# Node-query gate loop: the GpSimd addition of two product buffers is given up, and TensorE sums all four in two halves

## The chip, the cores and the metric

The kernel runs on one core of a Trainium2 chip, as one program. The metric is the device time in microseconds (us) from start to end; lower is better. The kernel before takes 1924.17 us, the median of 3 runs (1922.68 to 1926.9).

## The reference, cut to what matters

The program is eight layers on 256 nodes of 768 features. The change lies in the first one, `L0_gnn`, which runs a relational graph convolution and a query gate twice:

```python
hg = einsum('bnf,gf->bng', h3, Wg[:, :F])            # nodes:   8 graphs x 32 nodes x 768
qg = einsum('blf,gf->blg', q, Wg[:, F:]) + bg        # queries: 8 graphs x 64 queries x 768
attn = sigmoid(hg[:, :, None, :] + qg[:, None, :, :])   # 8 x 32 x 64 x 768
qi = einsum('bnlf,blf->bnf', attn, q)                # sum over the 64 queries
alpha = sigmoid(h3 @ Wq[:, :F].T + qi @ Wq[:, F:].T + bq)
hn = alpha * tanh(qi) + (1 - alpha) * h3
```

`attn` has 12.6 million elements in each of the two passes (l = 0, 1), and every one needs an addition, a sigmoid, a multiplication by q and a place in the sum over the queries.

## The kernel before

**Tiling.** A pass of the gate is a loop of 96 steps: 24 groups G (j = G // 8 is one of three blocks of 256 features, b = G % 8 is one graph) of four steps t, each for 16 of the graph's 64 queries. A step holds 128 partitions (8 nodes x 16 queries) x 1024 elements (4 sets of nodes x 256 features), in float32.

**One step.** TensorE fills two PSUM banks with node + query sums (`fill_pe`, L850: two bf16 products of 512 columns against a selection matrix; the rows come from the buffer `gate_rows`, kept as three bf16 parts). ScalarE takes the sigmoid into a product buffer (L969). VectorE multiplies by the query values `gate_queries`, in place (L1018, the helper's line is L120). TensorE sums over the queries with a selection matrix of 32 columns (`query_sum_pe`, L860: four column tiles of 256 columns, float32, one "quad" below; the profile records two matmuls for each float32 product), accumulating in bank 4 over all graphs of a block.

**Buffers.** There are two fill buffers in PSUM, so filling n waits for sigmoid n - 2 (`attended`), and eight product buffers (two groups), so the sigmoids of group G wait for the sums of group G - 2 (`qi_ps`, L967). The query values stand in three buffers (RBUF), so those of group G + 3 are requested once group G is multiplied (`weighed`, L728).

**The sum before.** GpSimd adds the second buffer of a group to the first (`gate_pool`, L1031), and TensorE sums three buffers, behind the third filling of the next group (L927 to L934). In the last group TensorE sums all four (L935).

**Beside the loop.** TensorE also works off products of the gate's weights (`beside`, L898): 36 products with the nodes and 24 with the query sums, of 128x256 float32 each, two or three behind the first filling of every group. The last 12 (features of block 2) come behind the loop (L943 to L949).

**Blocks.** Behind the sum of a block ScalarE copies it out, TensorE turns it (`turn_qi_pe`, in groups 9 and 17 behind the second filling, and behind the loop) and ScalarE copies it again.

**Transfers.** SyncE's queue issues all of them in program order: `gate_sp` (L793) the query parts to DRAM and back as rows, three buffers of query values, the node parts to DRAM and back; then a weight matrix of 2304 KB (L1041, L1045); then `gate_loop_sp` (L816), for each group the query values of G + 3 and the rows of G + 8, and in group 16 one more weight matrix.

The order of work on each engine is written out by hand; engines meet by semaphores (`mark`, `at`) alone.

Of the kernel before, what the change touches and what calls it, by code (L numbers as in the profile page):

```python
# [10 lines left out]
ALU = mybir.AluOpType  # L11
# [4 lines left out]
T = 256  # L16
TC = T // P
D = 768
DC = D // P
# [20 lines left out]
class Counts:  # L40
# [20 lines left out]
    def at(self, name, key=0):  # L61
        if self.counted:
            return self.sem(name), self.value[name, key]
        return self.sem(name), 1
# [104 lines left out]
def build(nc, dram, out_dram):  # L169
    ctx = ExitStack()  # L170
    with ctx:
# [61 lines left out]
        def loaded(key):  # L233
            return at(f"slot{counts.slot.get(key, 0)}_loaded", key)
# [558 lines left out]
        def gate_sp(q, l):  # L793
            load(q, ("Wgh", l), dram["L0_gnn_Wg"][0])
            load(q, ("Wqh", l), dram["L0_gnn_Wq"][0])
            load(q, ("Wqi", l), dram["L0_gnn_Wq"][1])
            counts.slot["work", l] = q.turns.pop(0)[0]
            at_wgh = [key for slot, key in q.turns].index(("Wgh", l))
            q.turns.append((q.turns.pop(at_wgh)[0], ("Wqi", l)))
            q.turns.append((counts.slot["work", l], ("Wqi", l)))  # L800
            if l == 0:
                for b in range(QB):
                    if b % 2 == 0:
                        query_parts_sp(q, b // 2)
                    query_rows_sp(q, 0, b)
            for G in range(RBUF):
                queries_sp(q, l, G)
            for b in range(QB):
                q.wait_ge(*(at(f"gate_rows_{b % 2}", (l, b - 2, "nodes") if b >= 2 else (l, QB - 2 + b, "queries"))))
                if b == QB // TC:  # L810
                    q.wait_ge(*at("gate_rows_1", (l, b - 1, "nodes")))
                if b % (QB // TC) == 0:
                    node_parts_sp(q, l, b // (QB // TC))
                node_rows_sp(q, l, b)
# [61 lines left out]
        def gate_pe(pe, l):  # L876
            wgh, wqh, wqi = (w3(unit((n, l)), DC, D) for n in ("Wgh", "Wqh", "Wqi"))
            pe.wait_ge(*loaded(("Wgh", l)))
            for c in range(TC):
                if l == 0 and c:  # L880
                    pe.wait_ge(*at("split_rest", NQ - 2))
                for k in range(DC):
                    if c == 0:
                        pe.wait_ge(*at("hidden", (l, k)))
                    for h in range(2):
                        t = pe.mm(PS[:, hidden_bank(c) + h, 0:HALF], hT[:, k, c * P:(c + 1) * P],
                                  wgh[:, k, h * HALF:(h + 1) * HALF], k == 0, k == DC - 1)
                t.then_inc(*(mark("unit_free", ("Wgh", l)) if c else mark("node_ps", (l, "rows"))))

            def hidden_product(o, k):  # L890
                return pe.mm(PS[:, gate_bank(o), o % 2 * T:(o % 2 + 1) * T], wqh[:, k, o * P:(o + 1) * P], hT[:, k, :],
                             k == 0 and o % 2 == 0, False)

            def query_product(o, f):
                return pe.mm(PS[:, gate_bank(o), o % 2 * T:(o % 2 + 1) * T], wqi[:, f, o * P:(o + 1) * P], qiT[:, f, :],
                             False, f == DC - 1 and o % 2 == 1)

            def beside(i):  # L898
                if i < DC * DC:
                    if i == 2 * DC:  # L900
                        pe.wait_ge(*at("split_rest", (l, TC - 1, 1)))
                    t = hidden_product(i // DC, i % DC)
                    if i == DC * DC - 1:
                        t.then_inc(*mark("unit_free", ("Wqh", l)))
                else:
                    f, o = divmod(i - DC * DC, DC)
                    pe.wait_ge(*at("qi_act", (l, "T", f // 2)))
                    query_product(o, f)

            pe.wait_ge(*at("kept", "gate_sel"))  # L910
            pe.wait_ge(*loaded(("Wqh", l)))
            pe.wait_ge(*loaded(("Wqi", l)))
            for n in range(STEPS):
                G, t = divmod(n, NQL)
                j, b = divmod(G, QB)
                if t == 0:
                    pe.wait_ge(*at(f"gate_rows_{b % 2}", (l, G, "nodes")))
                fill_pe(pe, l, n)
                if t == 0:
                    for i in range((5 * G + 1) // 2, (5 * G + 6) // 2):  # L920
                        beside(i)
                elif t == 1 and b == 1 and j:
                    pe.wait_ge(*at("qi_act", (l, "sb", j - 1)))
                    for f in range(2):
                        m = turn_qi_pe(pe, f, QI_BANK, f * TILE)
                    m.then_inc(*mark("qi_ps", (l, "turned", j - 1)))
                elif t == 2 and G:  # L927
                    if b == 1 and j:
                        pe.wait_ge(*at("qi_act", (l, "T", j - 1)))
                    pe.wait_ge(*at("folded", (l, G - 1)))  # L930
                    pe.wait_ge(*at("weighed", (l, NQL * G - 1)))
                    for u in (0, 2, 3):
                        m = query_sum_pe(pe, l, G - 1, u)
                    m.then_inc(*mark("qi_ps", (l, G - 1)))  # L934
            for u in range(NQL):  # L935
                pe.wait_ge(*at("weighed", (l, STEPS - NQL + u)))
                m = query_sum_pe(pe, l, GROUPS - 1, u)
            m.then_inc(*mark("qi_ps", (l, GROUPS - 1)))
            pe.wait_ge(*at("qi_act", (l, "sb", NREL - 1)))
            for f in range(2):  # L940
                turn_qi_pe(pe, f, 2 * f, 0).then_inc(*mark("qi_ps", (l, "turned", NREL - 1 + f)))
            pe.wait_ge(*at("qi_act", (l, "T", NREL - 1)))
            for o in range(DC):  # L943
                query_product(o, DC - 2)
            pe.wait_ge(*at("qi_dve", (l, "T")))
            for o in range(DC):
                t = query_product(o, DC - 1)
                if o % 2:
                    t.then_inc(*(mark("node_ps", (l, o // 2)) if o < DC - 1 else mark("unit_free", ("Wqi", l))))  # L949

        def gate_act(a, l):
            for c in range(TC):
# [75 lines left out]
                v.then(v.tt(gth[:, o2, :], gth[:, o2, :], galpha[:, o2, :], ALU.mult))  # L1028
                v.tt(hT[:, o2, :], hT[:, o2, :], gth[:, o2, :], ALU.add).then_inc(*mark("gated", (l, g)))

        def gate_pool(g, l):  # L1031
            for G in range(GROUPS - 1):
                w = [products(l, NQL * G + t) for t in range(2)]
                g.wait_ge(*at("weighed", (l, NQL * G + 1)))
                g.tt(w[0], w[0], w[1], ALU.add).then_inc(*mark("folded", (l, G)))


        def L0_gnn_sp(q):
            start_sp(q)
            gate_sp(q, 0)  # L1040
# [31 lines left out]

        def L0_gnn_pool(g):
            norm_pool(g, "L0_gnn")
            for l in range(2):
                gate_pool(g, l)

        def L0_gnn_dve(v):
            start_dve(v)
# [2559 lines left out]
```

## Time and profile before

| | us |
|---|---|
| median of 3 runs | 1924.17 |
| profiled execution, its own time | 1920.13 |
| its span (first to last instruction) | 1918.0 |
| gate loop, pass 0: first to last multiplication | 168.3 to 330.4 |
| gate loop, pass 1 | 434.6 to 595.7 |
| TensorE matmul busy, whole span | 1730.7 (90%) |
| VectorE busy | 708.6 (37%) |
| ScalarE busy | 438.5 (23%) |
| GpSimd busy | 177.0 (9%) |

Engines in the profile: PE is TensorE's matmuls, PEld its weight loads, DVE VectorE, ACT ScalarE, POOL GpSimd, SPq the transfers that SyncE issues. The page's busy shares are means over eight layers; the change touches the two gate loops, some 160 us each, and these are to be read by themselves. The mean granted clock of TensorE over the span is 0.975.

### The profile page before, as it was taken

How to read it: one execution, taken by the hardware profiler on the slowest of the kernel's cores; microseconds unless marked ns; L12 is line 12 of the kernel's file. 1: busy time of each engine (PE TensorE's matmuls, PEld its weight loads, DVE VectorE, ACT ScalarE, POOL GpSimd, SP SyncE). 2: the span in 40 equal slices, each digit the busy share in tenths (PEclk: the TensorE clock that was granted, in tenths of full speed). 3: DMA queues.
4: the chain of work that ended last, by engine and by line, in shares of the span. 5: the costliest groups of instructions: out<-in, count | busy, mean ns of one | idle time of the engine just before them, and what ended most of it. 6: DMA issues, size and time to landing. Idle time of an engine off the chain costs nothing.

```text
span 1918.0 us, 26881 instructions
## 1 busy us (share of the span) xinstructions
PE 1730.7 (90%) x11856; PEld 1043.3 (54%) x11856; DVE 708.6 (37%) x1179; ACT 438.5 (23%) x816; POOL 177.0 (9%) x81
## 2 busy tenths in 40 slices
PE   7997867997767999999999998887999899999999
PEld 4674433573435655567764443333566555766666
DVE  4325998008997222154321000001423232234220
ACT  0014555115663111043311000000521010131110
POOL 0002443004441000000000000000002000000000
PEclk9999899999999999989989999999999999999999
DMA  9216653617544677730358999999734336212650
GB/s 376 99 45 210 149 142 122 246 46 197 143 156 163 237 309 297 284 144 6 143 197 356 418 428 429 428 428 429 300 149 168 114 135 261 83 66 108 264 223 18
DMA packets 80748, 408.25 MB, mean 213 GB/s; under 512 B 9768, under 2 KB 50240, under 8 KB 58992
## 3 DMA queue, kind: packets, MB, share of 16 engines
q1 hardware_dynamic: 76112, 402.41, 55.0%
q10 hardware_dynamic: 4512, 4.03, 0.7%
q8 instruction: 98, 1.61, 0.3%
q14 instruction: 26, 0.21, 0.0%
HBM read 400.85 MB, written 5.51 MB: 212 GB/s over the span
## 4 chain that ended last, share of the span: by engine, by line
PE 69%; DVE 13%; DMA 12%; issue 4%; ACT 2%; POOL 0%; SPq 0%; DVEq 0%; ACTq 0%
PE banks L114 67%; DVE weight_ring L120 10%; DMA weight_ring<-in_L_ffn_c_fc_dram 7%; PE banks L117 2%; DMA weight_ring<-in_L_gnn_W_in_dram 2%; DMA weight_ring<-in_L_ffn_c_proj_e_dram 1%; ACT weight_ring L148 1%; DVE stat L266 1%; DMA gate_queries<-in_L_gnn_query_rep_dram 1%; DVE xn_tok L125 0%; DMA node_parts<-gate_node_parts 0%; DMA ident<-in_c_ident_dram 0%; DVE xT L137 0%; DVE stat L268 0%; DVE rgat_xr L137 0%
## 5 line engine op out<-in xcount | busy, mean ns | idle before, releaser
L120 DVE TENSOR_TENSOR weight_ring<-weight_ring,gate_queries 128x1024 f32<-128x1024 f32 x192 | 308.2, 1675 | 17.4 <-ACT weight_ring L148 16.2
L114 PE MATMUL banks<-weight_ring,xT 128*128 128x384 f32 x864 | 292.3, 490 | 2.4 <-DVE rgat_xr L137 1.5
L114 PEld LDWEIGHTS banks<-weight_ring,xT 128*128 128x128 f32 x864 | 161.9, 191 | 109.6 <-issue 9.0
L148 ACT ACTIVATE weight_ring<-banks 128x1024 f32<-128x1024 f32 x192 | 185.5, 1026 | 134.5 <-PE banks L114 134.4
L120 POOL TENSOR_TENSOR weight_ring<-weight_ring 128x1024 f32<-128x1024 f32 x46 | 150.3, 3266 | 429.2 <-DVE weight_ring L120 429.2
L114 PE MATMUL banks<-xT,weight_ring 128*128 128x256 f32 x792 | 182.2, 385 | 3.2 <-ACT x_tok L151 3.2
L114 PEld LDWEIGHTS banks<-xT,weight_ring 128*128 128x128 f32 x792 | 153.3, 194 | 31.2 <-issue 7.3
L114 PE MATMUL banks<-weight_ring,selrow 128*32 128x256 f32 x1168 | 81.5, 413 | 79.3 <-DVE weight_ring L120 79.1
L114 PE MATMUL banks<-weight_ring,r_xd 128*32 128x384 f32 (+1 forms) x2304 | 142.7, 406 | 1.1 <-DVE r_xd L124 0.6
L114 PE MATMUL banks<-weight_ring,moe_xdT 128*64 128x384 f32 x720 | 122.0, 489 | 21.7 <-DMA weight_ring<-in_L_ffn_c_fc_dram 20.7
L114 PE MATMUL banks<-gate_rows,selrow 96*128 96x512 bf16 x384 | 112.5, 406 | 12.0 <-ACT weight_ring L148 6.8
L114 PEld LDWEIGHTS banks<-weight_ring,r_xd 128*32 128x32 f32 x2304 | 76.6, 110 | 64.2 <-issue 54.5
L137 DVE COPY y_tok<-banks 128x384 f32<-128x384 f32 x32 | 17.8, 557 | 248.7 <-PE banks L117 248.7
L114 PEld LDWEIGHTS banks<-weight_ring,selrow 128*32 128x32 f32 x1168 | 40.8, 114 | 116.8 <-issue 95.7
L114 PEld LDWEIGHTS banks<-weight_ring,moe_xdT 128*64 128x64 f32 x720 | 50.6, 137 | 89.6 <-issue 54.9
L114 PE MATMUL banks<-weight_ring,y_tok 128*64 128x384 f32 x504 | 85.9, 490 | 10.9 <-DMA weight_ring<-in_L_ffn_c_proj_e_dram 10.9
L148 ACT ACTIVATE moe_h_tok<-banks 128x384 f32<-128x384 f32 x32 | 15.7, 491 | 265.9 <-PE banks L114 265.9
L114 PE MATMUL banks<-weight_ring,r_hT 128*32 128x192 f32 (+1 forms) x1152 | 73.2, 407 | 1.0 <-ACT r_hT L151 1.0
L114 PEld LDWEIGHTS banks<-gate_rows,selrow 96*128 96x128 bf16 x384 | 30.2, 101 | 77.7 <-issue 33.3
L114 PEld LDWEIGHTS banks<-weight_ring,y_tok 128*64 128x64 f32 x504 | 34.3, 137 | 55.5 <-issue 38.9
L114 PEld LDWEIGHTS banks<-weight_ring,r_hT 128*32 128x32 f32 x1152 | 36.7, 110 | 37.2 <-issue 34.0
L120 DVE TENSOR_TENSOR selrow<-banks,gate_node_parts 128x384 f32<-128x384 f32 x16 | 8.5, 555 | 129.9 <-ACT gate_node_parts L151 99.9
(371 smaller groups left out, 1856.3 us busy)
## 6 DMA issues: line engine op xcount, KB each, us to landing
weight_ring<-in_L_ffn_c_fc_dram SPq DMA_DIRECT2D x30, 2304.0 KB, 23.8
weight_ring<-in_L_ffn_c_proj_e_dram SPq DMA_DIRECT2D x21, 2304.0 KB, 28.3
gate_queries<-in_L_gnn_query_rep_dram SPq DMA_DIRECT2D x48, 512.0 KB, 4.0
weight_slot_heads<-in_L_ffn_c_proj_e_dram SPq DMA_DIRECT2D x9, 2304.0 KB, 28.3
weight_ring<-in_L_ffn_w_gate_dram SPq DMA_DIRECT2D x8, 2304.0 KB, 9.4
weight_ring<-in_L_ffn_w_up_dram SPq DMA_DIRECT2D x8, 2304.0 KB, 9.1
weight_ring<-in_L_ffn_w_down_dram SPq DMA_DIRECT2D x8, 2304.0 KB, 9.2
weight_ring<-in_L_ffn_w_dram SPq DMA_DIRECT2D x16, 1152.0 KB, 8.2
```

Source lines behind the costliest of these rows:

```text
L114: return self.e.matmul(out, lhsT, rhs, start=start, stop=stop)
L117: return self.e.transpose(out, src, self.ident[0:n, 0:n])
L120: return self.e.tensor_tensor(out, a, b, op)
L137: return self.e.tensor_copy(out, a)
L148: return self.e.activation(out, a, f, **kw)
L266: t = v.e.bn_stats(half_stats[:, c, h, :], src[:, 2 * c + h, :])
```

## The change

GpSimd's addition goes (`gate_pool` and the wait `folded`). TensorE sums the first two buffers of the last group behind the second filling of a group, and the other two behind the fourth; in groups 9 and 17, where the second filling is followed by the turn of a block, all four behind the fourth. Six of the `beside` products go ahead of the loop, 52 into it (13 per 6 groups), and two behind it. Behind the loop the last 12 products are ordered by pairs of output chunks, so that the first pair is complete after four. In pass 0 SyncE requests the three buffers of query values before the query rows of graphs 6 and 7.

```diff
@@ gate_sp: transfers ahead of the loop
                 for b in range(QB):
+                    if b == QB - 2:
+                        for G in range(RBUF):
+                            queries_sp(q, l, G)
                     if b % 2 == 0:
                         query_parts_sp(q, b // 2)
                     query_rows_sp(q, 0, b)
-            for G in range(RBUF):
-                queries_sp(q, l, G)
+            else:
+                for G in range(RBUF):
+                    queries_sp(q, l, G)
@@ gate_pe
             pe.wait_ge(*loaded(("Wqh", l)))
+            if l == 0:
+                pe.wait_ge(*at("split_rest", (NQ - 1, "biased")))
+            for i in range(DC):
+                beside(i)
             pe.wait_ge(*loaded(("Wqi", l)))
             for n in range(STEPS):
...
                 fill_pe(pe, l, n)
                 if t == 0:
-                    for i in range((5 * G + 1) // 2, (5 * G + 6) // 2):
+                    for i in range(DC + 13 * G // 6, DC + 13 * (G + 1) // 6):
                         beside(i)
-                elif t == 1 and b == 1 and j:
+                if t == 1 and b == 1 and j:
...
-                elif t == 2 and G:
+                elif t == 1 and G:
+                    pe.wait_ge(*at("weighed", (l, NQL * G - 3)))
+                    for u in range(2):
+                        query_sum_pe(pe, l, G - 1, u)
+                elif t == 3 and G:
                     if b == 1 and j:
                         pe.wait_ge(*at("qi_act", (l, "T", j - 1)))
-                    pe.wait_ge(*at("folded", (l, G - 1)))
                     pe.wait_ge(*at("weighed", (l, NQL * G - 1)))
-                    for u in (0, 2, 3):
+                    for u in range(0 if b == 1 and j else 2, NQL):
                         m = query_sum_pe(pe, l, G - 1, u)
                     m.then_inc(*mark("qi_ps", (l, G - 1)))
...
             m.then_inc(*mark("qi_ps", (l, GROUPS - 1)))
+            for i in range(DC + 13 * GROUPS // 6, (DC - 2 + DC) * DC):
+                beside(i)
...
-            for o in range(DC):
-                query_product(o, DC - 2)
-            pe.wait_ge(*at("qi_dve", (l, "T")))
-            for o in range(DC):
-                t = query_product(o, DC - 1)
-                if o % 2:
-                    t.then_inc(*(mark("node_ps", (l, o // 2)) if o < DC - 1 else mark("unit_free", ("Wqi", l))))
+            for g in range(DC // 2):
+                for f in (DC - 2, DC - 1):
+                    if f == DC - 1:
+                        pe.wait_ge(*at("qi_dve", (l, "T")))
+                    for o in (2 * g, 2 * g + 1):
+                        t = query_product(o, f)
+                t.then_inc(*(mark("node_ps", (l, g)) if g < DC // 2 - 1 else mark("unit_free", ("Wqi", l))))
@@ gate_pool, and its call in L0_gnn_pool
-            for G in range(GROUPS - 1):
-                w = [products(l, NQL * G + t) for t in range(2)]
-                g.wait_ge(*at("weighed", (l, NQL * G + 1)))
-                g.tt(w[0], w[0], w[1], ALU.add).then_inc(*mark("folded", (l, G)))
```

## Rows read from the trace of the kernel before

**Rows 1.** The chain of waits, 0 to 700 us, in pass 0: start, length, what.
```profile
257.31 4.30 DVE weight_ring L120 x4
...
261.61 2.40 issue
```

**Rows 2.** The instructions on the product buffers, 224 to 297 us: durations min/median/max in ns.
```profile
L120 DVE TENSOR_TENSOR weight_ring<-weight_ring,gate_queries x44: 1210/1212/3372, 223.8 to 294.2; 128x1024 f32<-128x1024 f32 x44
...
L120 POOL TENSOR_TENSOR weight_ring<-weight_ring x11: 3263/3266/3268, 226.2 to 293.2; 128x1024 f32<-128x1024 f32 x11
```

**Rows 3.** The timeline, 244 to 258 us: start, length, engine, operation, [idle before it].
```profile
244.14 1.50 PE L114 MATMUL banks<-weight_ring,selrow 128*32 128x256 f32 x24 [2.02 <-DVE weight_ring L120]
...
245.57 1.04 PE L114 MATMUL banks<-gate_rows,selrow 96*128 96x512 bf16 x4
...
246.45 1.46 PE L114 MATMUL banks<-xT,weight_ring 128*128 128x256 f32 x6
...
247.74 1.07 PE L114 MATMUL banks<-gate_rows,selrow 96*128 96x512 bf16 x4
...
252.92 3.77 ACT L148 ACTIVATE weight_ring<-banks 128x1024 f32<-128x1024 f32 x4 [2.60 <-PE banks L114]
```

**Rows 4.** The timeline, 428 to 485 us: VectorE behind one transfer, in pass 1.
```profile
457.09 10.18 DVE L120 TENSOR_TENSOR weight_ring<-weight_ring,gate_queries 128x1024 f32<-128x1024 f32 x7 [1.17 <-DMA gate_queries<-in_L_gnn_query_rep_dram]
```

**Rows 5.** The timeline at the end of pass 1, 584 to 650 us.
```profile
581.07 14.61 DVE L120 TENSOR_TENSOR weight_ring<-weight_ring,gate_queries 128x1024 f32<-128x1024 f32 x9
...
591.29 1.50 PE L114 MATMUL banks<-weight_ring,selrow 128*32 128x256 f32 x24 [2.02 <-DVE weight_ring L120]
...
592.72 0.60 PE L114 MATMUL banks<-gate_rows,selrow 96*128 96x512 bf16 x2
...
593.26 1.07 PE L114 MATMUL banks<-weight_ring,selrow 128*32 128x256 f32 x16
...
596.44 0.59 ACT L151 COPY selrow<-banks 128x512 f32<-128x512 f32 x1 [2.05 <-PE banks L114]
...
597.08 1.16 PE L114 MATMUL banks<-ident,selrow 128*128 128x128 f32 x8 [0.71 <-ACT selrow L151]
...
598.25 5.45 PE L114 MATMUL banks<-gate_qiT,weight_ring 128*128 128x256 f32 x24
...
602.95 0.69 DVE L120 TENSOR_TENSOR xn_tok<-xn_tok,gate_queries 128x512 f32<-128x512 f32 x1 [2.81 <-ACT gate_queries L148]
```

**Rows 6.** Three stretches: busy us (and starts) of each engine, granted clock, DMA share, GB/s.
```profile
177.00:183.70 6.70, 6.27 (x38) 3.21 (x38) 5.46 (x5) 2.63 (x3) 3.27 (x1) 0.75 0.82 263
257.50:284.30 26.80, 18.95 (x156) 10.35 (x157) 26.80 (x17) 16.12 (x18) 13.06 (x4) 1.00 0.54 138
350.00:361.00 11.00, 11.00 (x36) 6.50 (x35) 0.00 (x0) 1.50 (x2) 0.00 (x0) 1.00 1.00 417
```

**Rows 7.** The chain of waits, 0 to 700 us: two transfers that the work waited for.
```profile
157.54 6.29 DMA node_parts<-gate_node_parts
...
445.73 11.34 DMA gate_queries<-in_L_gnn_query_rep_dram
```

**Rows 8.** Transfers issued at 179.1, 449.3, 170.0 and 297.6 us: KB, us to landing.
```profile
gate_queries<-in_L_gnn_query_rep_dram SPq DMA_DIRECT2D x1, 512.0 KB, 10.6
...
gate_queries<-in_L_gnn_query_rep_dram SPq DMA_DIRECT2D x1, 512.0 KB, 11.7
...
node_parts<-gate_node_parts SPq DMA_DIRECT2D x1, 576.0 KB, 3.3
...
gate_queries<-in_L_gnn_query_rep_dram SPq DMA_DIRECT2D x1, 512.0 KB, 4.0
```

**Rows 9.** The timeline of pass 0: first filling, the request behind group 2, last multiplication.
```profile
166.53 0.59 PE L114 MATMUL banks<-gate_rows,selrow 96*128 96x512 bf16 x2 [4.20 <-DMA gate_rows<-node_parts]
...
190.42 0.35 SPq L154 DMA_DIRECT2D gate_queries<-in_L_gnn_query_rep_dram  x1
...
329.17 1.23 DVE L120 TENSOR_TENSOR weight_ring<-weight_ring,gate_queries 128x1024 f32<-128x1024 f32 x1 [1.38 <-ACT weight_ring L148]
```

More of the change, by code:

```diff
@@ L1029, in gate_dve @@
                 v.tt(hT[:, o2, :], hT[:, o2, :], gth[:, o2, :], ALU.add).then_inc(*mark("gated", (l, g)))
-        def gate_pool(g, l):
-            for G in range(GROUPS - 1):
-                w = [products(l, NQL * G + t) for t in range(2)]
-                g.wait_ge(*at("weighed", (l, NQL * G + 1)))
-                g.tt(w[0], w[0], w[1], ALU.add).then_inc(*mark("folded", (l, G)))
         def L0_gnn_sp(q):
@@ L1074, in L0_gnn_pool @@
             norm_pool(g, "L0_gnn")
-            for l in range(2):
-                gate_pool(g, l)
         def L0_gnn_dve(v):
```

## The prediction

> **What bounds the kernel now.** I read the page's busy shares first (in the table above). They say TensorE, but they are means over eight layers; the change touches two loops of 160 us, so these are read alone. The chain of waits, cut to a loop, is VectorE's: in a group of 6.70 us it holds four multiplications for 4.30 us and an "issue" stretch of 2.40 us that belongs to VectorE too [rows 1]. The windows confirm it: between 257.5 and 284.3 us VectorE is busy for all 26.8 us, TensorE for 18.95, ScalarE for 16.12, at a granted clock of 1.00 and a DMA share of 0.54 [rows 6].
>
> Then the instructions on the product buffers: the same multiplication takes 1212 ns as a rule and 3372 ns at most; one GpSimd addition lasts 3266 ns [rows 2]. Their records overlap a little, so I take the spacing s of a fast one and x of the slow one from two counts. A group is 3s + x = 6.70. Seven multiplications behind the transfer at 457.09, one of them slow, take 10.18 us, the last one with its full 1.21: 5s + x = 8.97 [rows 1, 2, 4]. So s = 1.135 and x = 3.295: VectorE loses 2.16 us in each group in which GpSimd works, 23 groups in each of two passes. Without that, VectorE needs 4s = 4.54 us for a group.
>
> **The change part by part.**
>
> *GpSimd's addition goes.* VectorE's bound falls from 6.70 to 4.54 us. If nothing else bounded, 46 x 2.16 = 99 us would go. It doesn't all go, for two reasons below.
>
> *TensorE's bill for a group, the term that decides.* At the high clock: two fillings start 0.88 us ahead of what follows them (245.57 to 246.45), so 0.44 each; six records, that is three beside products, 1.29 us (246.45 to 247.74), 0.43 each [rows 3]. Three quads last 1.50, two 1.07: 0.43 each [rows 5]. Around the quads there are gaps. Three quads are 1.29 us, but the filling behind them starts after 1.43 (244.14 to 245.57 and 591.29 to 592.72): 0.14 on the way out. A filling is 0.44, but the quads behind that of 592.72 start after 0.54, with their data ready: 0.10 on the way in [rows 3, 5]. Now: 4 x 0.44 + 3 x 0.43 + 2.5 x 0.43 + 0.24 = 4.37 us, inside 6.70, with an idle time of 2.02 ahead of the sum [rows 3]. After: 4 x 0.44 + 4 x 0.43 + 13/6 x 0.43 + 2 x 0.24 = 1.76 + 1.72 + 0.93 + 0.48 = 4.89 us. That is above VectorE's 4.54, so TensorE becomes the bound. Bounds: 4.55 if the gaps are hidden in a full queue (then VectorE bounds), 5.37 if each gap is twice as long, since the way in rests on one place. I take 4.89, from the nearest rows.
>
> The Trainium skill, TensorEngine Tiling (Array Packing), Key Properties, says that a change of tiling mode drains TensorE; here the mode (128x32 against full width) changes four times in a group in place of two. It agrees with the two gaps, gives no figure, and speaks against splitting the sum in halves: with one block of four quads the bill would be 4.65.
>
> *Do the waits fit in between?* ScalarE needs 3.77 us for four sigmoids [rows 3], so it isn't the bound. A sigmoid starts 0.65 us behind its filling (252.27 to 252.92 in the loop, the filling of rows 3 one group on). The quads behind the second filling wait for the second multiplication of the group before, which is two fillings further back than what they'd wait for behind the fourth. The quads behind the fourth filling wait for the fourth multiplication, and ScalarE, which needs them to refill the buffers, is by then two or three steps ahead of VectorE. Queued behind a quad that waits are the next filling, its sigmoid and all beside products; with VectorE 0.35 us per group faster than TensorE that wait is empty after the first groups. Cost taken: 0, ends 0 and 0.3 us a group.
>
> *Turns of a block, groups 9 and 17.* All four quads stand behind the fourth filling there, beside 1.16 us of turning [rows 5], less the gaps of one block: about 1.2 us each where TensorE bounds; 2.4 per pass.
>
> *The first three groups win nothing.* In pass 1 the query values of group 3 are issued at 445.73, behind the weight matrix, and land 11.34 us later, at 457.07; VectorE starts group 3 at 457.09, on that landing [rows 4, 7]. Neither transfer is moved in pass 1, and its issue follows SyncE's rows, not VectorE. Faster, VectorE would want it at about 449 (434.6 + 3 x 4.9). So group 3 starts at 457.1 as before. Group 4's values land at 449.3 + 11.7 = 461.0 [rows 8], in time for 457.1 + 4.6. In pass 0 the values requested at 179.1 land 10.6 us later, at 189.7 [rows 8]; group 3 started at 190.4, where SyncE's next request shows group 2 done [rows 9]. The new place of the first three requests spares the node parts the transfers beside them: 6.29 us in place of 3.3 [rows 7, 8]; but they now delay the query parts and the rows of graphs 6 and 7, for which SyncE waits before the node parts. I take 0.5 us (ends -1 and 3): group 3 at 189.2. Later the lead of a request is two groups, 9.8 us, against a landing of 4.0 [rows 8], and the DMA share of 0.54 x 6.70 = 3.6 us a group stays under 4.89.
>
> *From group 3 to the end.* When group 3 starts, TensorE has filled up to step 17 of 0 to 95 and waits for group 3's second multiplication, 2.3 us off. Then 78 fillings, 19.25 groups to the start of the last: 19.25 x 4.89 = 94.1; the turns 2.4; from the last filling 0.65 + 1.02 + 0.1 + 1.21, and 0.7 of queueing: 3.7. Sum 102.5 us. Now it is 595.68 - 457.09 = 138.6 in pass 1 [rows 4, 5] and 330.40 - 190.4 = 140.0 in pass 0 [rows 9].
>
> *The clock.* Where TensorE idled, the granted clock fell (0.75 over 177.0 to 183.7, half of it at the low level of 1.2 GHz); under unbroken work it stays 1.00 (350 to 361) [rows 6]. The stall ahead of group 3 will bring one such fall per pass: half of 6.7 us at half speed loses 1.7; I take 1.5.
>
> So pass 1 ends at 457.1 + 104.0 = 561.1, 34.6 earlier; pass 0 at 189.2 + 104.0 = 293.2, 37.2 earlier.
>
> *Behind the loop.* Two beside products (0.86) stand in the 0.64 from ScalarE's copy to the turn (596.44 to 597.08) and its release before: 0.15 late, ends 0 and 0.5. The first output pair is complete after 4 products in place of 8, 1.7 us earlier; but the pass goes on only when TensorE is through all 12 (5.45 us from 598.25) or VectorE's chain, begun at 602.95, is done [rows 5]. I take a gain of 1.1 for each pass, ends 0 and 2. Both together: 1.9 us.
>
> *Six products ahead of the loop.* In pass 0 TensorE idles 4.20 us there [rows 9], and they take 2.6: hidden. In pass 1 they delay the first filling by about 1.5 us, covered by the wait for group 3.
>
> **Sum.** 37.2 + 34.6 + 1.9 = 73.7 us. The profiled execution took 1920.13, so 1846.4; it lies 4.0 under the median of the runs, which gives 1924.2 - 73.7 = 1850.5. What follows starts at PE-bound stages or at loads released by them, and moves with them. I forecast 1850.
>
> **Rivals.**
> A. *The gaps close, VectorE bounds.* 4.54 in place of 4.89: 2 x 19.25 x 0.35 = 13 us less, and the clock's 3 perhaps: 1835. For it: the gaps may be the wait's own cost. Against: at 591.29 nothing was waited for on the way out [rows 5]. 15%.
> B. *More gap, or late query values.* At 5.37 a group 18.5 us more: 1869. If landings of 11.7, as beside a weight matrix [rows 8], held for the whole loop, two groups would take 11.7, one 5.85: 2 x 21 x 0.96 = 40 more, 1890; against it the 4.0 of the later ones. Together 14%.
> C. *Slower than before: TensorE at its low level for the loop.* All products last twice as long: 8.8 + 0.5 = 9.3 us a group, 2 x 21 x 2.6 = 109 us more: 2033. It is slower than before once a share f of over 0.41 of the loop is at the low level (4.89 + 4.4 f > 6.70). For it: the falls now. Against: they follow idle times of 2 us a group, which the change takes away, and 350 to 361 holds 1.00 [rows 6]. 3%.
> D. *VectorE isn't slow for GpSimd's sake.* Then 6.70 stays and the time with it: 1922. Against: exactly one multiplication in each group is slow, as one addition is made in each [rows 1, 2]. The Trainium skill, SBUF — State Buffer, Who interferes with whom, says that a VectorE instruction with two SBUF inputs and a GpSimd one that reads SBUF exclude each other on a shared port; the trace agrees, 1.135 + 2.16 = 3.3 being the GpSimd record's 3.27. 2%.
> The forecast has 66%.
>
> **Range and chances.** What a measurement of this kernel can tell from no change is about 0.2%, 4 us. A to B's first half and the ends of the small terms (start -1 to 3, tail 4, waits 0.3 x 40) give 1834 to 1872, with under 2 in 10 outside. Faster: all but C and D, 0.95; same 0.02; slower 0.03.
>
> **What would show it.** No multiplication over 1.3 us. From group 3 on a period near 4.9, TensorE busy for nine tenths or more at clock 1.00, and quads in two blocks with 0.1 and 0.14 of gap; a period of 4.55 with VectorE unbroken is A, one over 5.2 is B. VectorE idle ahead of group 3 in both passes, released by the query values' DMA; if it isn't there, the start-up term was wrong. Loops from group 3 to the end of about 104 us.

## The result, and the profile after

The kernel after takes **1856.88 us**, the median of 4 runs (1853.85 to 1860.77); the kernel before took 1923.6 in the 4 runs counted with it (1922.68 to 1926.9). The ratio is 0.9651, with a 95% interval from 0.9627 to 0.9676: 3.5% faster, 66.7 us. The prediction was 1850 within 1834 to 1872. The profiled execution took 1854.55 us, its span is 1852.4.

The chain of waits, 0 to 700 us (start, length, what): the loops, which were VectorE's [rows 1], are now unbroken stretches of TensorE, ahead of each a wait for query values.

```profile
179.76 12.44 DMA gate_queries<-in_L_gnn_query_rep_dram
...
194.64 98.72 PE banks L114 x878
...
412.22 11.01 DMA gate_queries<-in_L_gnn_query_rep_dram
...
425.67 97.62 PE banks L114 x878
```

The instructions on the product buffers, 225 to 285 us (durations min/median/max in ns), against [rows 2]: no slow multiplication is left.

```profile
L120 DVE TENSOR_TENSOR weight_ring<-weight_ring,gate_queries x49: 1218/1220/1226, 224.4 to 284.4; 128x1024 f32<-128x1024 f32 x49
```

The timeline of one group in that loop, against [rows 3]. Each gap is read as the distance of two starts less the work between (a half sum is 16 records, a filling 2, a beside product 2).

```profile
237.34 1.07 PE L114 MATMUL banks<-weight_ring,selrow 128*32 128x256 f32 x16
...
238.35 1.04 PE L114 MATMUL banks<-gate_rows,selrow 96*128 96x512 bf16 x4
238.99 3.06 ACT L148 ACTIVATE weight_ring<-banks 128x1024 f32<-128x1024 f32 x3 [0.52 <-PE banks L114]
...
240.04 4.63 DVE L120 TENSOR_TENSOR weight_ring<-weight_ring,gate_queries 128x1024 f32<-128x1024 f32 x4 [0.18 <-ACT weight_ring L148]
...
240.32 0.60 PE L114 MATMUL banks<-gate_rows,selrow 96*128 96x512 bf16 x2
...
240.76 1.03 PE L114 MATMUL banks<-xT,weight_ring 128*128 128x256 f32 x4
...
241.62 0.60 PE L114 MATMUL banks<-gate_rows,selrow 96*128 96x512 bf16 x2
...
242.15 1.07 PE L114 MATMUL banks<-weight_ring,selrow 128*32 128x256 f32 x16
...
243.15 1.04 PE L114 MATMUL banks<-gate_rows,selrow 96*128 96x512 bf16 x4
...
244.12 1.07 PE L114 MATMUL banks<-weight_ring,selrow 128*32 128x256 f32 x16
...
245.12 0.60 PE L114 MATMUL banks<-gate_rows,selrow 96*128 96x512 bf16 x2
```

A group with two beside products lasts 240.32 to 245.12 = 4.80 us; one with three has 0.43 more, 5.23. VectorE waits 0.2 to 0.3 us a group for ScalarE, and ScalarE for TensorE's fillings. Four stretches in one view (length, then busy us and starts of PE, PEld, DVE, ACT and POOL, granted clock, DMA share, GB/s), against [rows 6]:

```profile
190.00:200.00 10.00, 5.36 (x36) 1.62 (x36) 7.78 (x7) 1.94 (x2) 0.00 (x0) 0.51 1.04 235
200.00:210.00 10.00, 10.00 (x90) 4.82 (x90) 8.48 (x8) 6.97 (x8) 0.00 (x0) 0.97 0.68 176
210.00:290.00 80.00, 80.00 (x739) 38.74 (x728) 75.44 (x65) 67.18 (x72) 0.00 (x0) 1.00 0.73 201
...
433.00:520.00 87.00, 87.00 (x803) 41.88 (x796) 81.93 (x71) 72.84 (x77) 0.00 (x0) 1.00 0.64 188
```

TensorE is busy all of the time at a granted clock of 1.00; VectorE for 94% of it. The clock is 0.51, that is nearly all at the low level of 1.2 GHz, in the first ten us. TensorE stood still there up to 194.64, for 6.39 us, since VectorE had no query values, and then worked at the low level. In the next ten the clock is 0.97. The first half sum behind this wait, and behind the one of 5.01 us in pass 1, lasts 1.93 and 1.85 us where the one at 237.34 takes 1.07:

```profile
194.64 1.93 PE L114 MATMUL banks<-weight_ring,selrow 128*32 128x256 f32 x16 [6.39 <-DVE weight_ring L120]
...
425.67 1.85 PE L114 MATMUL banks<-weight_ring,selrow 128*32 128x256 f32 x16 [5.01 <-DVE weight_ring L120]
```

VectorE ahead of group 3 in either pass (timelines), against [rows 4, 9]:

```profile
192.22 8.04 DVE L120 TENSOR_TENSOR weight_ring<-weight_ring,gate_queries 128x1024 f32<-128x1024 f32 x7 [8.60 <-DMA gate_queries<-in_L_gnn_query_rep_dram]
```

```profile
423.25 11.68 DVE L120 TENSOR_TENSOR weight_ring<-weight_ring,gate_queries 128x1024 f32<-128x1024 f32 x10 [7.22 <-DMA gate_queries<-in_L_gnn_query_rep_dram]
```

The end of pass 1 in the timeline, against [rows 5]:

```profile
526.78 0.64 PE L114 MATMUL banks<-weight_ring,selrow 128*32 128x256 f32 x8 [0.50 <-DVE weight_ring L120]
...
527.49 0.58 ACT L151 COPY selrow<-banks 128x512 f32<-128x512 f32 x1 [2.23 <-PE banks L114]
...
528.32 1.05 PE L114 MATMUL banks<-ident,selrow 128*128 128x128 f32 x8
...
529.39 5.45 PE L114 MATMUL banks<-gate_qiT,weight_ring 128*128 128x256 f32 x24
...
534.67 2.74 PE L114 MATMUL banks<-x_tok,ident 128*128 128x384 f32 x8
...
536.47 0.69 DVE L120 TENSOR_TENSOR xT<-xT,xn_tok 128x512 f32<-128x512 f32 x1
...
537.25 2.84 PE L114 MATMUL banks<-ident,xT 128*128 128x128 f32 x24
...
538.79 1.03 DVE L266 BATCH_NORM_STATS2 stat<-banks 128x6 f32<-128x384 f32 x2 [1.35 <-PE banks L114]
```

And one place far behind the change. It is the turn from the first mixture layer to the next one. First the kernel before, then the one after:

```profile
837.18 0.30 PE L114 MATMUL banks<-small 64*64 64x24 f32 x4 [1.47 <-issue]
...
837.41 1.56 PE L114 MATMUL banks<-before,ident 128*128 128x256 f32 x6
```

```profile
767.39 0.30 PE L114 MATMUL banks<-small 64*64 64x24 f32 x4 [0.70 <-issue]
...
773.87 2.72 PE L114 MATMUL banks<-before,ident 128*128 128x256 f32 x6 [6.18 <-issue]
```

TensorE stands still for 0.70 and 6.18 us for nothing that the profile shows ("issue"), where it waited 1.47 at the same turn before. The six products behind it last 2.72 us in place of 1.56, at a lower clock (0.72 over 774 to 780 us).

**Where the 65.6 us of span went** (before less after; a pass is cut at the first multiplication of group 3 and at the end of the last one, and the layers behind begin at the first BATCH_NORM behind pass 1; group 3 of pass 0 before is counted at 190.4, as in the prediction, and its record starts at 190.32):

| stage | predicted | measured |
|---|---|---|
| start of the program to group 3 of pass 0 | 1.2 | -1.8 |
| group 3 to the end, pass 0 | 36.0 | 35.4 |
| end of pass 0 to group 3 of pass 1 | 0.95 | 0.2 |
| group 3 to the end, pass 1 | 34.6 | 35.1 |
| end of pass 1 to the layers behind | 0.95 | 0.1 |
| everything behind | 0 | -3.4 |
| sum | 73.7 | 65.6 |

### The profile page after: what moved, and what is told of

Read it like the earlier page. It is cut to its first block, busy times and chain, and to the rows that moved or that the text cites. A ratio compares the mean times of both kernels' runs of the same rounds, so it can differ in the third digit from the quotient of the medians.

```text
span 1852.4 us, 27529 instructions
## 1 busy us (share of the span) xinstructions
PE 1738.4 (94%) x12224; PEld 1040.0 (56%) x12224; DVE 624.6 (34%) x1179; ACT 444.2 (24%) x816; POOL 26.7 (1%) x35
## 4 chain that ended last, share of the span: by engine, by line
PE 81%; DMA 12%; DVE 5%; issue 1%; ACT 1%; SPq 0%; POOL 0%; DVEq 0%; ACTq 0%
PE banks L114 79%; DMA weight_ring<-in_L_ffn_c_fc_dram 6%; PE banks L117 2%; DMA weight_ring<-in_L_ffn_c_proj_e_dram 2%; DMA weight_ring<-in_L_gnn_W_in_dram 2%; DVE weight_ring L120 1%; DMA gate_queries<-in_L_gnn_query_rep_dram 1%; DVE stat L266 1%; DVE xn_tok L125 0%; DMA query_parts<-gate_query_parts 0%; DMA ident<-in_c_ident_dram 0%; DVE xT L137 0%; ACT weight_ring L148 0%; DMA node_parts<-gate_node_parts 0%; DVE rgat_xr L137 0%
## 5 line engine op out<-in xcount | busy, mean ns | idle before, releaser
L120 DVE TENSOR_TENSOR weight_ring<-weight_ring,gate_queries 128x1024 f32<-128x1024 f32 x192 | 223.7, 1221 | 31.6 <-DMA gate_queries<-in_L_gnn_query_rep_dram 15.8
L148 ACT ACTIVATE weight_ring<-banks 128x1024 f32<-128x1024 f32 x192 | 191.0, 1024 | 57.8 <-PE banks L114 54.7
L114 PE MATMUL banks<-weight_ring,selrow 128*32 128x256 f32 x1536 | 104.5, 392 | 12.5 <-DVE weight_ring L120 12.4
L114 PEld LDWEIGHTS banks<-weight_ring,y_tok 128*64 128x64 f32 x504 | 34.3, 137 | 55.8 <-issue 39.6
L120 DVE TENSOR_TENSOR r_h<-banks,r_silu 128x256 f32<-128x256 f32 (+2 forms) x32 | 13.3, 416 | 111.1 <-PE banks L114 78.7
```

What stands on the lines that cost most here:

```text
L114: return self.e.matmul(out, lhsT, rhs, start=start, stop=stop)
L120: return self.e.tensor_tensor(out, a, b, op)
L148: return self.e.activation(out, a, f, **kw)
```

## The experiments

Stages are compared by two times: from the first filling to the end of the last multiplication of a pass, and from group 3 to that end. The first is 163.9 and 162.2 us (pass 0, pass 1) before, and 128.9 and 126.4 after; the second is 140.0 and 138.6 before, 104.6 and 103.5 after.

### The addition alone goes, nothing takes its place

The kernel before, without GpSimd's addition:

```diff
-                    pe.wait_ge(*at("folded", (l, G - 1)))
...
-                g.tt(w[0], w[0], w[1], ALU.add).then_inc(*mark("folded", (l, G)))
```

> The kernel before without GpSimd's addition, and without the buffer that it would have carried: three of four buffers are summed in each group but the last, so a quarter of the query sum is left out. Theory (GpSimd's reads block VectorE's multiplications): no multiplication lasts over 1.3 us, VectorE's spacing of 1.135 sets a group of 4.54 us with TensorE's bill at 4.37, 98 us from group 3 to the end of each pass in place of 139, time about 1843. Rival (VectorE is slow for another reason): slow multiplications of 3.3 us stay, and the time stays at 1923.

Measured: 1846.5 us, ratio 0.9593 (0.9565 to 0.962). The busy times of 30 us of its loop:

```profile
230.00:260.00 30.00, 28.67 (x244) 14.62 (x246) 29.76 (x27) 25.57 (x28) 0.00 (x0) 1.00 0.75 197
```

It leaves a quarter of the query sum out, so that it is no way to compute the layer. Its multiplications take 1218 ns, 1226 at most. VectorE is busy 29.76 of 30 us and TensorE 28.67: here VectorE bounds, at four unhindered multiplications a group. From group 3 to the end it takes 100.4 and 100.5 us, expected 98; in 3.5 and 3.7 of them VectorE waits for ScalarE. So the fold had cost 39.6 and 38.1 us a pass, and the change gives 3 to 4 of them back, since TensorE sums the fourth buffer and switches twice more.

### GpSimd reads SBUF again, for nothing

The kernel after, with one GpSimd product of 128x1024 a group on data of its own, for which nobody in the loop waits:

```diff
+                    g.wait_ge(*at("weighed", (l, NQL * G + 1)))
...
+                    g.tt(own, own, bc(ones[:].unsqueeze(1), [P, 8, P]), ALU.mult).then_inc(*mark("private", (l, G)))
```

> The changed kernel, and GpSimd multiplies 128x1024 elements of the adjacency counts by ones in each group of both loops, in place, at the moment at which it added before; nobody in the loop waits for it. Theory (exclusive blocking while both read SBUF): the slow multiplications of 3.3 us are back, VectorE bounds at 6.7 us a group in place of 4.88, about 1.8 x 21 x 2 = 76 us more than the changed kernel, 1933. Rival (what cost before was TensorE's wait for the addition, not the port): 1857, multiplications at 1.21.

Measured: 1925.29 us, ratio 1.0019 (1.0006 to 1.0032): the whole gain is gone, though TensorE's order and its waits are those of the kernel after. The instructions on the product buffers, the GpSimd product in the timeline, and VectorE in pass 1:

```profile
L120 DVE TENSOR_TENSOR weight_ring<-weight_ring,gate_queries x37: 1210/1212/3393, 224.0 to 284.3; 128x1024 f32<-128x1024 f32 x37
```

```profile
231.94 3.29 POOL L120 TENSOR_TENSOR A_ds<-A_ds,ones 128x1024 f32<-128x1024 f32 x1 [3.43 <-DVE weight_ring L120]
...
243.07 1.07 PE L114 MATMUL banks<-weight_ring,selrow 128*32 128x256 f32 x16 [1.39 <-DVE weight_ring L120]
...
245.37 3.27 POOL L120 TENSOR_TENSOR A_ds<-A_ds,ones 128x1024 f32<-128x1024 f32 x1 [3.43 <-DVE weight_ring L120]
```

```profile
454.55 138.71 DVE L120 TENSOR_TENSOR weight_ring<-weight_ring,gate_queries 128x1024 f32<-128x1024 f32 x84 [0.92 <-DMA gate_queries<-in_L_gnn_query_rep_dram]
```

The median is 1212 ns and the maximum 3393, where [rows 2] have 1212 and 3372. VectorE runs without a break for 138.7 us, the kernel before's 138.6, and TensorE idles 1.39 us ahead of a half sum. This settles rival D: it was GpSimd's use of SBUF, not the wait nor the order on TensorE.

### GpSimd writes only

The same place, a memset of 128x768 in place of the product:

```diff
+                    g.wait_ge(*at("weighed", (l, NQL * G + 1)))
...
+                    g.e.memset(selrow_flat[:, 0:D], 0.0).then_inc(*mark("private", (l, G)))
```

> The changed kernel, and GpSimd fills 768 elements of a free buffer with zeros at the same moment of each group: it writes and doesn't read. Theory (only reads block): 1857, multiplications at 1.21. Rival (any GpSimd access blocks VectorE): some 0.8 us longer multiplications, 4.54 + 0.8 = 5.3 us a group in place of 4.88, 18 us more, 1875.

Measured: 1856.59 us, ratio 0.966 (0.9643 to 0.9677), the kernel after's own. The grouped view of GpSimd in 225 to 285 us shows the twelve memsets at work, and the multiplications beside them take no notice, though a block of only 0.7 us would show in the maximum:

```profile
L1088 POOL MEMSET selrow<- 128x768 f32 x12 | 8.8, 737 | 50.9 <-DVE weight_ring L120 50.9
```

```profile
L120 DVE TENSOR_TENSOR weight_ring<-weight_ring,gate_queries x49: 1216/1219/1227, 223.9 to 283.9; 128x1024 f32<-128x1024 f32 x49
```

The Trainium skill (SBUF — State Buffer, Who interferes with whom) says that a VectorE instruction with two SBUF inputs contends with a GpSimd one that reads SBUF, and not with one that only writes it. Both halves of it agree with these two runs: 1925.29 against 1856.59. It gives no price for the first; here it is 2.16 us of VectorE's time for each 128x1024 product: in the run with the product, pass 1 has 64 fast multiplications and 20 slow ones in 138.71 us, and with the spacing of 1.135 for the fast ones a slow one takes 3.30.

### One block of four quads in place of two halves

In the kernel after, all sums stand behind the fourth filling:

```diff
-                elif t == 1 and G:
-                    pe.wait_ge(*at("weighed", (l, NQL * G - 3)))
-                    for u in range(2):
-                        query_sum_pe(pe, l, G - 1, u)
...
-                    for u in range(0 if b == 1 and j else 2, NQL):
+                    for u in range(NQL):
```

> The changed kernel with all four quads in one block behind the fourth filling of every group. Theory of the bill alone (two changes of tiling mode less, 0.25 us a group): 4.63 us a group, 10 us less, 1847. Rival, my theory now: a block of four (1.72 us and the gaps) holds the next filling back longer than ScalarE's lead, ScalarE runs dry and the fillings behind are late in turn; about 5.3 us a group, 20 us more, 1877.

Measured: 1877.39 us, ratio 0.9765 (0.9748 to 0.9783): 20 us slower than two halves, though two changes of mode a group are spared. A group in the timeline:

```profile
241.10 0.61 PE L114 MATMUL banks<-gate_rows,selrow 96*128 96x512 bf16 x2 [0.63 <-ACT weight_ring L148]
241.63 1.45 PEld L114 LDWEIGHTS banks<-weight_ring,selrow 128*32 128x32 f32 x32 [0.42 <-issue]
...
243.50 0.11 PEld L114 LDWEIGHTS banks<-gate_rows,selrow 96*128 96x128 bf16 x2 [0.41 <-DMA gate_rows<-query_parts]
...
244.20 1.02 ACT L148 ACTIVATE weight_ring<-banks 128x1024 f32<-128x1024 f32 x1 [1.33 <-PE banks L114]
...
245.44 2.86 ACT L148 ACTIVATE weight_ring<-banks 128x1024 f32<-128x1024 f32 x3 [0.22 <-PE banks L114]
...
246.52 0.60 PE L114 MATMUL banks<-gate_rows,selrow 96*128 96x512 bf16 x2 [0.64 <-ACT weight_ring L148]
```

The four quads are one block (241.63 to 243.50). While it runs TensorE fills nothing, so ScalarE waits 1.33 us for the next filling; then TensorE waits 0.64 us for ScalarE to free a fill buffer. There are only two. A group lasts 241.10 to 246.52 = 5.42 us where the bill of the work alone is 4.65. With half sums no pause between fillings is as long: the wait of ScalarE behind one is 0.52 us (238.99 in the kernel after). That is what the split buys, and 0.24 us of gaps is its price.

The same block behind the *third* filling, in the kernel before without GpSimd:

```diff
-                    pe.wait_ge(*at("folded", (l, G - 1)))
-                    for u in (0, 2, 3):
+                    for u in range(NQL):
```

> The kernel before without GpSimd's addition, TensorE sums all four buffers in one block behind the third filling; nothing else changed. TensorE's bill is 4.37 + 0.43 = 4.80 us a group, 0.08 under the changed kernel's 4.88. Theory of the bill alone: 102 us from group 3 to the end, 1856. Rival, that a block of four starves ScalarE: 107 to 108 us, 5 more in each pass, 1866.

Measured: 1868.62 us, ratio 0.9718 (0.9688 to 0.9748), 5.03 us a group (its blocks start at 239.49 and 244.52), from group 3 to the end 109.5 and 109.4 us. In 30 us:

```profile
230.00:260.00 30.00, 29.10 (x274) 14.66 (x266) 27.65 (x25) 23.26 (x26) 0.00 (x0) 1.00 0.70 185
```

Neither engine is full: 29.10 and 27.65. Behind the block ScalarE waits for a filling, and then TensorE for ScalarE, each for less time than with the block behind the fourth:

```profile
242.00 3.78 ACT L148 ACTIVATE weight_ring<-banks 128x1024 f32<-128x1024 f32 x4 [0.93 <-PE banks L114]
...
243.99 0.60 PE L114 MATMUL banks<-gate_rows,selrow 96*128 96x512 bf16 x2 [0.30 <-ACT weight_ring L148]
```

Of the three kernels that sum four buffers, the one with two halves is the fastest, by some 12 and 20 us. The 20 are the block's alone. The 12 aren't: this run has the kernel before's 2.5 beside products a group in place of 13/6, which is 0.14 us more, some 3 us a pass, and the old tail and place of the requests. Of the difference 4.9 and 5.9 us lie between group 3 and the end of a pass. So what the block behind the third filling costs by itself isn't shown; by these numbers it is nearer 2 to 3 us a pass.

### The tail's order and the place of the requests, undone

The kernel after with the old order of the last 12 products and with SyncE's requests for query values behind all query rows:

```diff
-            for g in range(DC // 2):
-                for f in (DC - 2, DC - 1):
+            for o in range(DC):
+                query_product(o, DC - 2)
...
-                    if b == QB - 2:
-                        for G in range(RBUF):
-                            queries_sp(q, l, G)
```

> The changed kernel with the last 12 products in their old order and the first three requests in their old place. As the prediction priced them: 1.1 us for each pass's tail and 0.5 for the requests, 1.9 + 0.5 = 2.4 more than the changed kernel, 1859. As the trace after reads (from the last multiplication to the next stage 8.8 and 12.1 us as before): the products' order is worth no more than 0.9, the two beside products behind the loop having taken it back; 1857 to 1858.

Measured: 1861.51 us, ratio 0.969 (0.9664 to 0.9716). The kernel after's interval ends at 0.9676, so the time doesn't tell the two apart. The stages tell more: last multiplication to the next stage (in pass 0 the first product `weight_ring,xT`, in pass 1 the first BATCH_NORM) 8.9 us in pass 0 and 12.2 in pass 1, against 7.9 and 12.1. So the order of the products is worth 1.0 us in pass 0 and about 0.2 in pass 1. The first filling of pass 0 comes 21.6 us behind the first of the 48 products `weight_ring,xT` ahead of the loop, against 19.0 after and 19.8 before; but group 3 starts all the same when its values land:

```profile
193.13 12.58 DVE L120 TENSOR_TENSOR weight_ring<-weight_ring,gate_queries 128x1024 f32<-128x1024 f32 x11 [3.04 <-DMA gate_queries<-in_L_gnn_query_rep_dram]
```

That is 0.9 us later than 192.22, and VectorE has waited 3.04 us for it, not 8.60. An earlier first filling is lost in a longer wait for group 3. Pass 0 even ends no later: at 295.27 us, against 296.80 and 295.34 in the two profiled executions of the kernel after. So the new place of the requests brought the first filling forward and no time that can be seen.

### The weight matrix behind group 5's requests

The kernel after; the first weight matrix of a loop goes into the loop's own list:

```diff
-            load(q, ("rel", 1, 0), dram["L0_gnn_W_rel2"][0])
...
-            load(q, ("L0g", 0), dram["L0_ffn_w_gate"][0])
...
+                if G == 5:
+                    load(q, *first)
```

> The changed kernel with the first weight matrix of each loop (2304 KB) requested behind group 5's requests in place of ahead of all. Theory (the wait for group 3's query values stands behind that matrix): they land about 4 to 6 us after their request, VectorE doesn't idle the 8.6 and 7 us ahead of group 3, and the fall of the clock behind it goes; some of the lead that TensorE won in the wait is lost. 12 to 15 us less than the changed kernel, 1843. Rival (the start is held by the rows' transfers or SyncE's order whatever the matrix does): 1857.

Measured: 1842.26 us, ratio 0.9589 (0.9564 to 0.9614); 1843 was expected. The chain of waits:

```profile
172.63 112.23 PE banks L114 x1018
...
403.55 5.63 DMA gate_queries<-in_L_gnn_query_rep_dram
...
427.70 13.72 DMA gate_queries<-in_L_gnn_query_rep_dram
```

Pass 0 is one stretch of TensorE from the start, 119.7 us from first filling to last multiplication. In pass 1 the values of group 3 land in 5.63 us in place of 11.01. But those requested behind the matrix at its new place land after 13.72, and VectorE waits 4.63 us for them: the same collision, moved.

### Both matrices in six pieces

The kernel of the last run; each matrix goes in six transfers of 384 KB over six groups, and group 3's values ahead of the node rows of graphs 6 and 7:

```diff
+                if b == QB - 2:
+                    queries_sp(q, l, RBUF)
...
-                if G + RBUF < GROUPS:
+                if G and G + RBUF < GROUPS:
...
-                if G == 5:
-                    load(q, *first)
-                if G == 2 * QB:
-                    load(q, *early)
+                for G0, unit_ in ((5, first), (2 * QB, early)):
+                    if G0 <= G < G0 + 6:
+                        load_piece(q, *unit_, G - G0)
```

> As e7_weights_later, but each of the two weight matrices of a loop is requested in six pieces of 384 KB, one behind the requests of each of six groups, and group 3's query values are requested ahead of the last node rows. In e7 pass 1 still has VectorE idle by 1.66 us at group 3 and by 4.63 us behind the matrix (landing 13.7 us against a lead of 9.8). Theory: both go, the loop is TensorE's from the first group in both passes; pass 1 falls from 122.2 to about 119.7 us from first filling to last multiplication, as pass 0: 2 to 4 us less than e7, 1839. Rival (many small requests crowd the transfer queue and the rows come late): 1842 or more.

Measured: 1840.44 us, ratio 0.9569 (0.9552 to 0.9585). Both passes take 119.7 us. The wait table, 130 to 560 us (in total, times, longest):

```profile
DVE weight_ring L120 <- DMA gate_queries<-in_L_gnn_query_rep_dram: 2.6, 4, 1.4
```

2.6 us in both passes, where two waits alone were 15.8. The pieces slow the query values too, but for more groups and each by less: a request at 449.4 us, among the pieces, lands after 11.2 us and few waits come of it. The time moves little against the last run (the intervals overlap), and the stall behind the mixture layer is there still:

```profile
756.93 2.72 PE L114 MATMUL banks<-before,ident 128*128 128x256 f32 x6 [6.02 <-issue]
```

### The length of TensorE's stream

Nothing but small products without effect is added to the last kernel, four of 128x8 ahead of each loop:

```diff
+            for _ in range(4):
+                pe.mm(PS[:, QI_BANK, 0:8], ident[:], before[:, 0, 0:8], True, True)
```

> As e8, with four small products (128x8) more ahead of each loop, for nothing but the length of TensorE's instruction stream. In the changed kernel and in all experiments with its number of TensorE instructions (12224 matmuls) TensorE stands still for 5.9 to 6.9 us, waiting for nothing visible, shortly behind the branch that ends the first mixture layer; before and e1 (11856) it didn't. If that is a matter of where the code lies, the wait may change its length with the padding; if it belongs to the 2304 KB transfer issued there, it stays at 6. Time as e8 or up to 4 us less.

> As e9, with twelve small products ahead of each loop. Code position: a wait of another length than in e8 or e9. Transfer: 6 us again. Time as e8, plus about 1 us for the padding, or up to 4 us less.

Measured: 1835.14 us with four, ratio 0.954 (0.9521 to 0.9558), the lowest median here, and 1839.59 with twelve, ratio 0.9559 (0.9534 to 0.9583). The same turn with four:

```profile
751.73 0.30 PE L114 MATMUL banks<-small 64*64 64x24 f32 x4 [1.20 <-issue]
```

With four and with twelve the stall is gone (1.20 and 1.21 us of waiting at that turn, and none behind it). It doesn't hang on the change's work, then, nor on the weight transfers of that turn, which are the same in all. From the end of the products `weight_ring,shared_h` to the first product `xT,gat_vec` the turn takes 12.6 us without padding and 6.3 with four. Yet everything behind pass 1 is only 1.7 us shorter (1313.6 against 1315.2), and the times of these two and of the last overlap in their intervals. So it isn't shown that taking the stall away gives back its 6 us.

### The kernel after once more

> The changed kernel once more, beside e8 on the same chip: 0.965 of the kernel before.

Measured: 1858.28 us, ratio 0.966 (0.9643 to 0.9677), with a stall of 7.03 us at that turn. All eight kernels with 12224 matmuls show one of 6.0 to 7.0; the two with 11856 (before, and the one without any addition) show 1.5 and 1.3, the two with padding 1.2. So it goes with the number of instructions ahead of that turn, and not with what they compute. What TensorE waits for there no run shows; that it is the fetching of its own instructions is a guess.

## Why the prediction was right, point by point

*VectorE's price.* The count from two spacings gave 2.16 us lost per addition. The slow multiplications are gone, and a GpSimd product that reads SBUF brought 3393 ns and the old 138.7 us back. Right.

*TensorE's bill, the term that decides.* 4.89 us a group forecast; 4.80 with two beside products and 5.23 with three make 4.87 over six groups, one of them with three. The gaps are 0.09 on the way in (a filling is 0.44, and the sum starts 0.53 behind that of 241.62) and 0.15 on the way out (a half is 0.86, and the filling starts 1.01 behind the sum of 237.34). From one place each in [rows 3, 5] they came out within 0.02. Rival A, that they close, is wrong: TensorE has no idle time and they stay.

*The rule on draining* (the Trainium skill, TensorEngine Tiling (Array Packing), Key Properties). The section says that a change of mode drains TensorE, and the gaps agree. My use of it misled: "with one block of four quads the bill would be 4.65" counts the work alone. The run with one block took 5.42 a group, since with two fill buffers a long block starves ScalarE. What I had left out in weighing it is who is fed by TensorE in between.

*Group 3 as the start.* Forecast: it starts on the landing of its values, 457.1 in pass 1, as late as before. It does: VectorE waited 8.60 and 7.22 us, landings 12.44 and 11.01. (The first multiplication of pass 1 before is at 435.69, not at 434.6, which is the first sigmoid; VectorE would then want group 3 at 450 in place of 449, and the landing still decides.) In pass 0 it came at 192.2 in place of 189.2. The untouched start of the program was 2.3 us later in that execution; of this the new order ahead of the loop made up 1.6, so that the request came 0.7 later than before (179.76), but its landing took 12.44 us in place of 10.6, and the 0.5 us that I had counted on the requests' new place didn't come. The two runs on transfers show what was left there: 16 us (128.9 and 126.4 down to 119.7 twice).

*From group 3 to the end:* 104.0 forecast, 104.6 and 103.5 measured. The clock's 1.5 us in it can be read off: two half sums and two fillings between them span 1.01, 0.96 and 1.01 us at the high level (183.37 to 186.35), and 5.55 us behind the wait of pass 0 (194.64 to 200.19), so 2.6 are lost; in pass 1 a half sum and two fillings take 3.60 (425.67 to 429.27) in place of 1.97, so 1.6. Without these the passes are 102.0 and 101.9, where the sum had 102.5. So in pass 0 two small errors partly cancel, 0.5 too much work and 1.1 too little for the clock.

*The step that failed: behind the loop.* I took a gain of 1.1 us for each pass, less 0.15 for the two beside products; pass 0 had 0.9, pass 1 0.1. I had reasoned from VectorE's chain, begun at 602.95 in [rows 5], as the one that ends last. In pass 0 it was: with the old order TensorE idles 0.82 us there for it, and with the new one TensorE goes on as soon as it is through the 12 products. In pass 1 TensorE has the turning of `x_tok` behind them (534.67 to 537.41), and VectorE's last addition ends at 537.16, under that cover; VectorE's chain didn't set the end, so making it earlier gives nothing. And of pass 0's 0.9 only 0.2 was left at group 3 of pass 1, since that group starts on a transfer.

*What I didn't price: everything behind.* That what follows moves with the loops was nearly right: it took 3.4 us more of 1310. The stall is a term that the prediction doesn't have: 0.70 and 6.18 us of waiting in place of 1.47, and from the last product `weight_ring,shared_h` to the first `xT,gat_vec` 12.2 us in place of 6.3. But the whole stage came out between 1311.8 and 1320.7 in the profiled executions of the ten other kernels, with 1313.6, 1313.9 and 1316.6 in the three that have no stall, and at 1321.4 in the second one of the kernel after. The 1310.2 of the kernel before is the shortest of all thirteen, so 3.4 is within the stage's own spread.

The 8.1 us between the 1846.4 that the sum gave for a profiled execution and its 1854.55 are thus: group 3 of pass 0 3.0 later (a request 0.7 later, a landing 1.8 longer, 0.5 that were not gained), the loops 0.6 in pass 0 and -0.5 in pass 1, the tail and what it passes on 1.6, and the stage behind 3.4.

## What to carry to other kernels

When an engine's time drops, write the bill of the next one in starts and not in durations, with the gaps, and then ask which engine it feeds: four quads in one block had the smaller bill and cost 20 us more. A GpSimd helper that reads SBUF beside a two-input VectorE instruction is paid for in VectorE's time, here 2.16 us for a helper of 3.3, even where nobody waits for it. A loop that gets faster runs into the transfers ahead of it: here a weight matrix that nobody had waited for stood ahead of the query values, and moving it and cutting it in pieces gave some 16 us more, nearly 15 of them by the moving.

## What the runs showed of the hardware

- A 512 KB transfer requested within 0.5 us behind one of 2304 KB on the same queue lands after 9.8 us (pass 0 of the run without the addition) to 13.7 (the matrix behind group 5), and later in the loop after some 4 us [rows 8]; the large one in pieces of 384 KB leaves 2.6 us of waits in two passes.
- TensorE going into 32-column sums costs some 0.09 us and out of them 0.14 to 0.15, with nothing to wait for, at each of the four changes in the group from 240.32 to 245.12 (kernel after).
- Behind a standstill of 6.39 us, and behind one of 5.01, TensorE worked at the low level of its clock for 5.6 and 3.6 us, which cost 2.6 and 1.6 us.
- A GpSimd memset beside VectorE's two-input multiplications costs them nothing (1219 ns against 1220), a GpSimd product of 128x1024 costs 2.16 us each.
- The same code at a turn of the program idled TensorE for 1.2 to 1.5 or for 6 to 7 us; four small products ahead of each loop, without effect on what is computed, moved it from the one to the other.
